# A recommender kernel in which two rounds of outer products share one trip through PSUM, every other step

## The reference

```python
xk = x = e                                           # (B, F=16, E=256)
for i in range(3):
    z = einsum('bfe,bge->bfge', x, xk).reshape(B, F * F, E)
    z = einsum('bcl,oc->bol', swapaxes(z, 1, 2), Ws[i]) + bs[i][None, :, None]
    z = sum(relu(z), axis=-1)                        # (B, 16)
    outs.append(z)
    xk = broadcast_to(z[:, :, None], (B, F, E))
h = concatenate(outs + [dense_ctx], axis=1)          # (B, 64)
y = relu(relu(h @ W_top1 + b_top1) @ W_top2 + b_top2) @ W_top3
```

## Time and profile before

| | us |
|---|---|
| median of 3 runs (lowest, highest) | 630.85 (630.07, 631.62) |
| the profiled execution | 628.34 |
| span of its trace | 626.6 |
| TensorE busy | 575.6 (92%) |
| VectorE busy | 499.5 (80%) |
| GpSimd busy | 463.7 (74%) |
| ScalarE busy | 455.3 (73%) |

### The profile page before, as it was taken

The page is one execution under the profiler, slowest core; times in us unless marked ns, Lnnn a source line. Parts: engine busy times, 40 slices in busy tenths (PEclk is TensorE's granted clock), DMA queues, the critical chain, the costliest instruction groups (busy, mean ns, idle before and its releaser), DMA issues.

```text
span 626.6 us, 19391 instructions
## 1 busy us (share of the span) xinstructions
PE 575.6 (92%) x7936; PEld 328.8 (52%) x7936; DVE 499.5 (80%) x220; ACT 455.3 (73%) x1298; POOL 463.7 (74%) x565
## 2 busy tenths in 40 slices
PE   2878798999999999999999999999999999997776
PEld 1444454555646555564656555565556555554354
DVE  5999999999898988889898988889888888941000
ACT  2666777787878787877887787777878788765542
POOL 6999999999988788888888888788878787621000
PEclk9999999999999999999999999999999999999988
DMA  3322222222222212222212122212212222100000
GB/s 97 112 73 73 69 70 68 70 70 65 69 64 61 61 58 63 61 61 62 65 56 65 57 61 60 69 55 68 60 55 67 61 61 57 47 3 1 1 1 2
DMA packets 14794, 35.97 MB, mean 57 GB/s; under 512 B 5922, under 2 KB 6306, under 8 KB 14690
## 3 DMA queue, kind: packets, MB, share of 16 engines
q0 software_dynamic: 12288, 33.57, 18.8%
q1 hardware_dynamic: 2418, 1.16, 0.7%
HBM read 34.70 MB, written 0.01 MB: 55 GB/s over the span
## 4 chain that ended last, share of the span: by engine, by line
PE 82%; POOL 8%; issue 4%; ACT 3%; DMA 1%; DVE 1%; SPq 0%; POOLq 0%
PE sum_ps L503 35%; PE turn_ps L483 10%; PE wide_ps L555 10%; PE outer_ps L535 8%; PE wide_ps L572 6%; PE wide_ps L546 4%; POOL emb L257 4%; PE outer_ps L531 4%; PE wide_ps L563 3%; POOL prods L267 2%; POOL prods L217 2%; ACT relu_k L426 1%; PE sum_ps L521 1%; PE sum_ps L517 1%; DVE prods L217 1%
## 5 line engine op out<-in xcount | busy, mean ns | idle before, releaser
L217 DVE TENSOR_TENSOR prods<-turn_ps,emb_t 128x3360 f32<-128x3360 f32 x128 | 466.1, 3655 | 55.1 <-ACT emb_t L399 52.2
L257 POOL DMA_INDIRECT emb<-tables,rows_sb x256 | 252.2, 985 | 45.4 <-issue 34.5
L503 PE MATMUL sum_ps<-prods,w_sb 128*32 128x272 f32 x4096 | 265.0, 397 | 18.6 <-POOL prods L217 11.1
L503 PEld LDWEIGHTS sum_ps<-prods,w_sb 128*32 128x32 f32 x4096 | 136.4, 110 | 103.6 <-issue 39.6
L426 ACT ACTIVATE relu_k<-outer_ps 128x1024 f32<-128x1024 f32 x128 | 132.4, 1035 | 11.2 <-PE outer_ps L535 11.1
L416 ACT ACTIVATE relu<-sum_ps,bias_sb 128x120 f32<-128x120 f32 x256 | 90.6, 361 | 58.4 <-PE sum_ps L503 57.2
L267 POOL TENSOR_TENSOR prods<-emb_t 128x256 f32<-128x256 f32 x128 | 95.3, 745 | 46.3 <-ACT emb_t L399 45.1
L398 ACT COPY emb_t<-turn_ps 128x512 f32<-128x512 f32 x128 | 75.3, 589 | 71.3 <-PE turn_ps L483 71.3
L483 PE MATMUL turn_ps<-ident_sb,emb 128*128 128x128 f32 x512 | 84.6, 289 | 12.7 <-DMA emb<-tables,rows_sb 10.0
L483 PEld LDWEIGHTS turn_ps<-ident_sb,emb 128*128 128x128 f32 x512 | 55.1, 142 | 60.5 <-issue 57.6
L406 ACT ACTIVATE prods<-emb_t 128x512 f32<-128x512 f32 x128 | 81.5, 637 | 3.3
(11 more groups left out here) (41 smaller groups left out, 284.3 us busy)
## 6 DMA issues: line engine op xcount, KB each, us to landing
emb<-tables,rows_sb POOLq DMA_INDIRECT x256
w_sb<-w_top SPq DMA_DIRECT2D x1, 512.0 KB, 4.3
ids_sb<-ids_t SPq DMA_DIRECT2D x1, 128.0 KB, 2.1
h<-dense_t SPq DMA_DIRECT2D x1, 128.0 KB, 2.9
w_sb<-w_top SPq DMA_DIRECT2D x1, 128.0 KB, 3.1
ident_sb<-ident SPq DMA_DIRECT2D x1, 64.0 KB, 2.1
w_sb<-w_cols SPq DMA_DIRECT2D x1, 64.0 KB, 1.9
wp_sb<-w_proj SPq DMA_DIRECT2D x1, 32.0 KB
```

The source lines that it names most:

```text
L217: eng.tensor_tensor(out, every, shifted, ALU.mult).then_inc(done, 1)
L257: nc.gpsimd.indirect_dma_start(out=emb[:, k % EMB_RING, t * E:(t + 1) * E], out_offset=None, in_=tables, in_offset=bass.IndirectOffsetOnAx ...
L503: last = nc.tensor.matmul(sum_ps[s * 2 * F:(s + 1) * 2 * F, 0:SUM_COLS], w_sb[:, c, odd, :], x[:, c, 2 * s + odd, :, :], start=c == 0 and ...
```

## The change

Two rounds are done as one **turn**. A group has two turns per layer instead of four rounds, at every other slot, `ROUNDS[k] + 2 * q`: modulo 8 the slots 6 and 0 (layer 1) and 2 and 4 (layer 2). The odd slots have no round any more. In a turn the bias matmul of each bank writes all 512 columns (its moving operand is the 256 bias columns read twice), then four outer-product matmuls write the first halves of the four banks and four more the second halves, with other weights (`z_wide` of the next q). One relu of 2048 columns moves all four banks. `relu_k` has another order inside, and `fold` reads it accordingly. Waits on round numbers count turns. Positions in the order of each engine are kept otherwise.

```diff
+HALF_G = 2
+TURNS = G4 // HALF_G
-ROUND_ORDER = sorted((PER * g + ROUNDS[k] + q, k, g, q) for g in range(GROUPS) for k in range(2) for q in range(G4))
+ROUND_ORDER = sorted((PER * g + ROUNDS[k] + 2 * q, k, g, q) for g in range(GROUPS) for k in range(2) for q in range(TURNS))
...
-        relu_k = sb("relu_k", [P, 2, G4, J, F * F])
+        relu_k = sb("relu_k", [P, 2, TURNS, J, HALF_G, F * F])
...
-                nc.scalar.activation(relu_k[:, k, q, :, :], outer_ps[:, :, 0:F * F], ACT.Relu).then_inc(outer_relu, 1)
+                nc.scalar.activation(relu_k[:, k, q, :, :, :].rearrange("p j h n -> p (j h n)"),
+                                     outer_ps[:].rearrange("p j n -> p (j n)"), ACT.Relu).then_inc(outer_relu, 1)
...
+                b = bias_wide[:, k, :].rearrange("p (h n) -> p h n", h=1).broadcast_to([P, HALF_G, F * F])
                 for j in range(J):
-                    nc.tensor.matmul(outer_ps[:, j, 0:F * F], ones_sb[j * R:(j + 1) * R, :], bias_wide[j * R:(j + 1) * R, k, :],
+                    nc.tensor.matmul(outer_ps[:, j, :], ones_sb[j * R:(j + 1) * R, :], b[j * R:(j + 1) * R, :, :],
                                      start=True, stop=False)
                 y = proj_b[:, g % PT_RING, :].rearrange("p (f k o) -> p k f o", f=F, k=2)
-                for j in range(J):
-                    last = nc.tensor.matmul(outer_ps[:, j, 0:F * F], z_wide[j * R:(j + 1) * R, k, q, :],
-                                            y[j * R:(j + 1) * R, k, :, :], start=False, stop=True)
+                for h in range(HALF_G):
+                    for j in range(J):
+                        last = nc.tensor.matmul(outer_ps[:, j, h * F * F:(h + 1) * F * F],
+                                                z_wide[j * R:(j + 1) * R, k, q * HALF_G + h, :],
+                                                y[j * R:(j + 1) * R, k, :, :], start=False, stop=h == HALF_G - 1)
                 last.then_inc(outer_done, 1)
...
-                pe.wait_ge(outer_relu, ROUND_NO[k, g, G4 - 1] + 1)
+                pe.wait_ge(outer_relu, ROUND_NO[k, g, TURNS - 1] + 1)
                 for q in range(G4):
                     for j in range(J):
-                        last = nc.tensor.matmul(wide_ps[j * R:(j + 1) * R, 0:F * F], fold_sb[:], relu_k[:, k, q, j, :],
-                                                start=q == 0, stop=q == G4 - 1)
+                        last = nc.tensor.matmul(wide_ps[j * R:(j + 1) * R, 0:F * F], fold_sb[:],
+                                                relu_k[:, k, q // HALF_G, j, q % HALF_G, :], start=q == 0, stop=q == G4 - 1)
```

More of the change, by code:

```diff
@@ L287, in z_spread @@
                 if g > 0:
-                    pool.wait_ge(outer_done, ROUND_NO[k, g - 1, G4 - 1] + 1)
+                    pool.wait_ge(outer_done, ROUND_NO[k, g - 1, TURNS - 1] + 1)
                 z = z_cat[:, g % CAT_RING, k * F:(k + 1) * F].rearrange("p (q u a) -> p q u a", q=G4, u=1)
@@ L361, in turn_proj @@
                 if g >= PT_RING:
-                    dve.wait_ge(outer_done, ROUND_NO[1, g - PT_RING, G4 - 1] + 1)
+                    dve.wait_ge(outer_done, ROUND_NO[1, g - PT_RING, TURNS - 1] + 1)
                 nc.vector.transpose(proj_b[:, g % PT_RING, :].rearrange("p (f m) -> p f m", f=F),
```

## The result

The changed kernel takes 653.01 us (median of four runs, 652.24 to 656.42) against 630.8 us before: ratio 1.036, 95% interval 1.032 to 1.040. It is 22.2 us slower; the forecast was 651, 20.5 us slower. The profiled execution took 652.24 us, its span is 650.4.

What follows compares the result with a forecast made beforehand. TensorE's own instruction order was taken to bound the middle. Turns +29.2, slot 28 +0.5, slots 1, 3 and 7 -0.8, slot 5 -3.1 and tail -5.3 gave +20.5 us on 630.85: 651 us, range 641 to 661.

Steps and rivals of the forecast that it cites:

- The prediction's first reading: Slots 1, 3 and 7: the round is already free under ScalarE's sum_ps read; without it 3.36 us becomes 3.33.
- roughly 25 us: Bare slots 1, 3 and 7: TensorE would wait this long over the run for ScalarE's read, some 0.7 us each.
- The bound that I refused: Slots 1, 3 and 7: upper bound of the gain from losing a round, the full 0.66 us per slot.
- the rival at 627 us: Slots 1, 3 and 7 shrink by 0.66 us instead of 0.02, 24.3 us off; 5 in 100.
- The forecast of -0.02 per slot: Slots 1, 3 and 7 without their round: some 38 x 0.02, -0.8 us, priced from slot 20, which has no round.
- Two full rounds: Rival on a turn's cost on TensorE: 0.66 us more than a round, 5.8 us more in all, 657; 10 in 100.
- a free bias: Rival on a turn's bias matmuls: a turn costs only 0.44 us more than a round, 645 us; 12 in 100.
- bare weight reloads: Rival: a turn's two new weight reloads cost 0.186 us each, 0.37 more per turn, 671 us; 5 in 100.
- The new wait: Slot 5: hidden2 waits for hidden1's relus behind slot 4's turn relu, eating 0.40 of 0.66 us; -3.1 us over 12 slots.
- it starts 0.80 us after a round's first matmul, 1.35 after a turn's: Step for slot 5: when ScalarE's relu starts, used with its 1.88 us to time the hidden relus and hidden2.
- I let GpSimd's lateness hide a turn: Turns of slots 14 and 22 counted as free, since TensorE then waits over 1 us for GpSimd; 53 turns left.
- the mechanism that I had priced for slot 28 alone: Even slot with neither wide item nor hidden layer behind it: no cover for the turn's long relu on ScalarE; +0.5 us, once.

Runs made afterwards that it cites:

- ScalarE letting go early: Changed kernel, layer 0's two relus read a constant instead of sum_ps, last read and side copy come first, so layer 0 is not computed: 622.22 us, ratio 0.988.

## Why the prediction was right

**The free rounds.** The prediction's first reading, that in slots 1, 3 and 7 a round hides under ScalarE's read of the one `sum_ps` bank, carries the result, and three runs show it from three sides: taking those rounds out gains next to nothing (35.05 against 35.52, all of it slot 5), shortening the read gives the 0.7 us per slot that the change had hoped for, and putting the turns there costs 0.3 to 0.4 us each instead of 1.19. The waits for side copies in these slots, 26.3 us from 143 us on, are the "roughly 25 us" named beforehand. The bound that I refused, the full 0.66 back, and with it the rival at 627 us, fell.

The forecast of -0.02 per slot came out at 0 to +0.02 in slots 3 and 7 and at +0.06 in slot 1. The last read is not all that the sum waits for: the term of 0.28 from the end of the read to the next sum covers the end of slot 1's side copy (324.80 to 325.06), and slot 20, the row of the forecast, has no side copy. And in slot 1 ScalarE begins to read 0.13 us after the sum's end and not 0.07, with a gather running beside it:

```profile
301.81 0.99 POOL L259 DMA_INDIRECT emb<-tables,rows_sb  x1
...
302.40 0.36 ACT L418 ACTIVATE relu<-sum_ps,bias_sb 128x120 f32<-128x120 f32 x1 [0.89 <-PE sum_ps L506]
```

With that gather moved, the reading starts after 0.07 again and slot 1 takes 3.36 us.

**The turn.** 0.55 forecast, 0.53 measured, with the bias at 0.22 to the first product (305.63 to 305.85) as worked out. Two full rounds (0.66), a free bias (0.44) and bare weight reloads (0.37 more) are all excluded. The Trainium skill ("TensorE: Matmul & The Clock Gate", The mechanism) has the sentence that a weight load overlaps running matmuls only in another row group; by it the two further reloads should have shown, and the trace disagrees, with 16 products in 0.97 us (305.85 to 306.82), 0.24 per set of four, the change of tile included. The same section also lets a load into a background weight buffer go ahead of running matmuls, and with that the trace agrees.

**Slot 5.** The new wait was named right, behind the relu of slot 4's turn, and the run that moves that relu shows it. Its size was the term that was off: hidden2 was to come 0.40 us later and comes 0.61 later (2.58 us after the sum and not 1.97, of which TensorE idles 0.54), so that the slot gives 0.08 (5.05 to 4.97 us) and not 0.26. The step that failed was "it starts 0.80 us after a round's first matmul, 1.35 after a turn's": that came from rows of the tail, where no gathers run. In slot 4 of the stream it is 1.63:

```profile
314.71 0.39 PE L535 MATMUL outer_ps<-bias_wide,ones_sb 32*128 32x512 bf16 x4
...
316.34 1.88 ACT L428 ACTIVATE relu_k<-outer_ps 128x2048 f32<-128x2048 f32 x1 [0.53 <-PE outer_ps L540]
...
318.84 1.17 ACT L450 ACTIVATE h<-wide_ps,b_cols 128x128 f32<-128x128 f32 x4
```

Slot 5 follows that start: where the relu came 1.46 us after the turn (ScalarE letting go early) it takes 4.81, at 1.51 (gather moved) 4.86, at 1.63 4.97. Eleven slots, not the twelve of the forecast, have this form; with slot 125, which gave 0.37, they gave 1.3 us in place of 3.1.

**The relu** of 2048 columns: 1.88 forecast, 1.88 measured (1879 ns in the mean).

**The stream as a whole.** The last sum starts 30.0 us later than before (560.73 to 590.70); the terms summed to 25.8. Of the 4.2 between, 1.8 are slot 5; 1.5 are slots 1, 3 and 7, which grew by 0.7 in all and did not shrink by 0.8; 0.9 lie in slots 14 to 31; and 0.8 lie in slots 0 to 13, before the first round, where the change does nothing. The turns' 0.53 in place of 0.55 takes 0.8 off. In slots 14 to 31 I let GpSimd's lateness hide a turn, but the turn of slot 22 has no wide item behind it, and its relu then holds up ScalarE's next read: the mechanism that I had priced for slot 28 alone, at 0.5 us, where slot 29 in fact grew by 0.93 (3.33 to 4.26). The sum of slot 24 waits 1.86 us for it:

```profile
108.80 2.04 PE L506 MATMUL sum_ps<-prods,w_sb 128*32 128x272 f32 x32 [1.86 <-ACT own L421]
```

**The tail.** 32.4 us forecast from the last sum to the fold of slot 142; 32.3 measured:

```profile
590.70 2.00 PE L506 MATMUL sum_ps<-prods,w_sb 128*32 128x272 f32 x29
...
622.96 1.93 PE L561 MATMUL wide_ps<-relu_k,fold_sb 128*32 128x256 f32 x32 [0.72 <-ACT h L456]
```

From the last sum to the end of the span it is 59.7 us against 65.8: the tail is the only place where the change does what it is for, because there rounds wait for relus, and it gave 6.2 where I had 5.3. Stream and tail together are +23.8 us in the profiles, +22.2 in the medians, +20.5 forecast. The terms are terms of the profiles, so 3.3 us is what they missed; that the medians lie only 1.7 from the forecast is in part luck, as the profile of before was 2.5 us below its median and that of the changed kernel 0.8.

## What to carry to other kernels

An item's cost is what stands beside it: the same four matmuls and a relu are free in a slot where the engine would wait anyway and cost their full length in a slot whose wait something else already covers, and a change of tile more between items of one tile. Before merging work into fewer and larger pieces, find for each slot what ends last, and put the larger piece where the wait is; here that choice of one constant is worth some 39 us. And look for such a slot in the trace without the item (here slot 20 of the fill): it prices the removal before anything is built.

## What was not expected of the hardware

- A gather issued by GpSimd (0.98 us) goes with a late start of a waiting ScalarE instruction. In the stream of the changed kernel and of the run with the gather moved, where ScalarE itself was free in time, it was so: with a gather ending between 0.4 us before and 0.23 us after the moment at which the relu should start, the relu came 0.07 to 0.64 us late, 0.33 to 0.49 us after the gather's end; with a gather begun 0.85 to 0.97 us after the turn and still running it came 0.12 to 0.23 late; with one begun 1.13 us after the turn or later, or none near, it was on time to 0.01 us. The runs show that the lateness follows the gather, not through what.
- Between a sum and a projection or fold, which all use TensorE as 128 rows by 32 columns, a round costs 0.14 us more than its own 0.66: the follow-up without change of tile comes after 1.83 us and that with one after 1.97. Ahead of hidden1, on 64 rows by 128 columns, it costs 0.66 alone.
- Without the odd rounds the run's tail gained less than worked out: from the last sum to the end 55.5 us, against 65.8 before, 10 us and not 15. Its mean granted clock was 0.986 against 0.992, and the rows above put some 3 of the 5 us on items that ran at the lower level. What the rest is was not tried.
